# A decoder layer on one core: the order of pieces in the cross-attention

## What is computed

```python
q = jnp.einsum('btc,oc->bto', x, Wq) + bq            # x: (4, 1024, 256), 16 heads of 16
kv = jnp.einsum('bic,oc->bio', encoder_output, Wkv) + bkv   # 64 context vectors a batch
att = jnp.einsum('bhtd,bhid->bhti', q, k) * (1.0 / np.sqrt(D))
att = jax.nn.softmax(att, axis=-1)
y = jnp.einsum('bhti,bhid->bhtd', att, v)
y = y.transpose(0, 2, 1, 3).reshape(B, T, C)
return jnp.einsum('btc,oc->bto', y, Wo) + bo
```

## Time and profile before

| | us |
|---|---|
| median of 3 runs | 1554.58 |
| fastest and slowest run | 1554.28, 1557.01 |
| the profiled execution's own time | 1554.44 |
| its span, first to last instruction | 1552.5 |

### The profile page before, as it was taken

The page is one execution under the profiler, slowest core; times in us unless marked ns, Lnnn a source line. Parts: engine busy times, 40 slices in busy tenths (PEclk is TensorE's granted clock), DMA queues, the critical chain, the costliest instruction groups (busy, mean ns, idle before and its releaser), DMA issues. The chain is left out here.

```text
span 1552.5 us, 44246 instructions
## 1 busy us (share of the span) xinstructions
PE 1482.7 (96%) x18228; PEld 1091.7 (70%) x18228; DVE 1111.8 (72%) x1694; ACT 888.0 (57%) x1644; POOL 441.0 (28%) x633
## 2 busy tenths in 40 slices
PE   7999899978899999999999999999998999999997
PEld 4656666654536666666666666666657889999997
DVE  5787789857678898989898989898946633333332
ACT  2323677755638888888888888888882311111111
POOL 4110667644431111111111111111111124544543
PEclk9999999999999999999999999999999999999999
DMA  6000000002331111111111111111105765565562
GB/s 205 1 21 11 11 2 1 1 1 108 145 113 35 41 37 42 36 44 34 43 35 43 35 42 36 42 36 43 35 12 172 239 223 199 191 214 193 195 215 63
DMA packets 80078, 124.05 MB, mean 80 GB/s; under 512 B 22243, under 2 KB 46949, under 8 KB 79878
## 3 DMA queue, kind: packets, MB, share of 16 engines
q1 hardware_dynamic: 74262, 105.87, 22.7%
q0 software_dynamic: 5616, 15.34, 2.7%
HBM read 94.66 MB, written 26.08 MB: 78 GB/s over the span
## 5 line engine op out<-in xcount | busy, mean ns | idle before, releaser
L566 DVE TENSOR_REDUCE sb_m_mx<-banks 128x1 f32<-128x1024 f32 x512 | 603.9, 1220 | 76.6 <-PE banks L314 68.8
L485 ACT ACTIVATE sb_m_pT<-banks 128x512 f32<-128x512 f32 x1024 | 556.3, 595 | 110.6 <-PE banks L343 98.9
L343 PE MATMUL banks<-sb_m_q,sb_m_k 99*32 99x512 bf16 x4096 | 466.8, 380 | 2.2 <-DMA sb_m_q<-sb_m_mx_parts 1.3
L314 PE MATMUL banks<-sb_m_k,sb_m_q 96*32 96x512 bf16 x4096 | 359.9, 379 | 1.1 <-DMA sb_m_k<-k_parts 0.6
L358 PE MATMUL banks<-sb_m_pT,sb_m_v 128*32 128x256 f32 x4096 | 314.6, 379 | 0.7 <-ACT sb_m_pT L485 0.7
L343 PEld LDWEIGHTS banks<-sb_m_q,sb_m_k 99*32 99x32 bf16 x4096 | 178.6, 96 | 80.8 <-ACT sb_m_pT L485 6.1
L358 PEld LDWEIGHTS banks<-sb_m_pT,sb_m_v 128*32 128x32 f32 x4096 | 176.8, 109 | 58.9 <-ACT sb_m_pT L485 1.2
L314 PEld LDWEIGHTS banks<-sb_m_k,sb_m_q 96*32 96x32 bf16 x4096 | 159.0, 96 | 75.9 <-DVE sb_m_mx L566 6.3
L235 POOL CAST sb_m_mx_parts<-sb_m_mxT 8x128 bf16<-8x128 f32 x64 | 18.1, 283 | 574.8 <-issue 563.6
L2094 ACT ACTIVATE sb_e_hT<-banks 128x512 f32<-128x512 f32 x78 | 46.6, 597 | 234.8 <-PE banks L2052 234.8
L2052 PEld LDWEIGHTS banks<-sb_e_xT,w 128*128 128x128 f32 x1248 | 145.3, 192 | 3.4 <-DVE sb_e_xT L2104 1.5
(11 more groups left out here) (258 smaller groups left out, 1965.5 us busy)
## 6 DMA issues: line engine op xcount, KB each, us to landing
w<-in_w SPq DMA_DIRECT2D x47, 1024.0 KB, 5.1
sb_m_q<-q_parts SPq DMA_DIRECT2D x384, 32.0 KB, 1.8
sb_m_k<-k_parts SPq DMA_DIRECT2D x384, 32.0 KB, 1.8
q_parts<-sb_m_parts SPq DMA_DIRECT2D x24, 256.0 KB, 2.5
k_parts<-sb_m_parts SPq DMA_DIRECT2D x24, 256.0 KB, 2.4
X<-in_x SPq DMA_DIRECT2D x4, 1024.0 KB, 10.4
x_rows<-X SPq DMA_DIRECT2D x8, 512.0 KB, 8.5
z_rows<-sb_g_zs SPq DMA_DIRECT2D x8, 512.0 KB, 4.4
```

What stands on the lines that cost most here:

```text
L314: mm = pe.matmul(ps[2 * (k % 2) + h][c:c + 32, :], q_s[0:R, i, k * P + c:k * P + c + 32], k_s[0:R, i, h * 512:(h + 1) * 512], start=True, ...
L343: mm = pe.matmul(ps[rotating(use)][c:c + 32, :], k_s[:, i2, m * P + c:m * P + c + 32], q_s[:, i2, h * 512:(h + 1) * 512], start=True, stop ...
L485: act.activation(pT[:, m, h * 512:(h + 1) * 512], ps[rotating(f"b{m}{h}")][:, :], ACT.Exp).then_inc(exped, 1)
L566: dve.tensor_reduce(mx[:, par % 2, k:k + 1], pz[:, 2 * (k % 2):2 * (k % 2) + 2, :].rearrange("p q n -> p (q n)"), AX.X, ALU.max).then_inc( ...
```

## The change

Three orders change, and what goes with them:

- TensorE issues the scores of tile n + 1 instead of tile n at the head of slot n; those of tile 0 stand ahead of the loop.
- In a slot the turn now stands between scores and products, and the query between products and projection. Before, the query stood ahead of the products and the turn behind them. ScalarE's copies follow, and its normalization moves ahead of the copy of the products.
- VectorE computes the maxima of tile n ahead of the sums of tile n - 1. The subtraction stays behind them.

```diff
     def pieces_of(n):
         m = n // 2
         if n % 2 == 0:
-            first = [("query1", m + 1)] if m + 1 < PAIRS else []
-            return first, [("turn", m + 2)] if m + 2 < PAIRS else []
-        return [("query0", m + 2)] if m + 2 < PAIRS else [], []
+            queries = [("query1", m + 1)] if m + 1 < PAIRS else []
+            return [("turn", m + 2)] if m + 2 < PAIRS else [], queries
+        return [], [("query0", m + 2)] if m + 2 < PAIRS else []
...
+            score(0)
             for n in range(SLOTS):
-                if n < NT:
-                    score(n)
-                queries, turns = pieces_of(n)
-                for p in queries:
+                if n + 1 < NT:
+                    score(n + 1)
+                turns, queries = pieces_of(n)
+                for p in turns:
                     pe.wait_ge(piece_copied, NUMBER[p])
                     piece(p, ps[7])
                 if 0 <= n - 2:
                     products(n - 2)
-                for p in turns:
+                for p in queries:
                     pe.wait_ge(piece_copied, NUMBER[p])
                     piece(p, ps[7])
...
-                for p in queries:
+                for p in turns:
                     take(p, ps[7])
+                if g + 2 < NG:
+                    norm((g + 2) * GT + r)
                 if 0 <= n - 2:
                     act.wait_ge(pv, n - 1)
...
-                if g + 2 < NG:
-                    norm((g + 2) * GT + r)
-                for p in turns:
+                for p in queries:
                     take(p, ps[7])
...
+                if n < NT:
+                    dve.wait_ge(scores, n + 1)
+                    dve.tensor_reduce(mx[:, n % 2, :], sc, AX.X, ALU.max).then_inc(max_done, 1)
                 if 0 <= n - 1 < NT:
                     sums(n - 1)
                 if r == 0 and 0 < g and g + 2 < NG:
                     shift_of(g + 2)
                 if n < NT:
-                    sc = pz[:, 2 * (n % 2):2 * (n % 2) + 2, :].rearrange("p q (h n) -> p (q h) n", h=8)
-                    dve.wait_ge(scores, n + 1)
-                    dve.tensor_reduce(mx[:, n % 2, :], sc, AX.X, ALU.max).then_inc(max_done, 1)
                     need(dve, probsT, n - 1)
```

More of the change, by code:

```diff
@@ L1537, in _ @@
                 g, r = n // GT, n % GT
+                sc = pz[:, 2 * (n % 2):2 * (n % 2) + 2, :].rearrange("p q (h n) -> p (q h) n", h=8)
+                if n < NT:
+                    dve.wait_ge(scores, n + 1)
+                    dve.tensor_reduce(mx[:, n % 2, :], sc, AX.X, ALU.max).then_inc(max_done, 1)
                 if 0 <= n - 1 < NT:
```

## The result

The changed kernel took 1549.61 us (median of 11 runs, 1543.58 to 1553.04) against 1554.58 (11 runs, 1551.54 to 1557.21): a ratio of 0.9959, with 0.9950 to 0.9967 as its interval. That is 5.0 us faster: a small difference, but the interval leaves out 1. I had forecast 1.9 us less than the median before, too little to be told from no change.

A forecast was written before the change was run, and what follows sets the result against it. TensorE was taken to bound the pairs, and the ring of VectorE's sums, maxima, subtraction and ScalarE's exponential the last slots. Terms -2.6 + 0.1 + 2.5 + 0.4 - 2.1 = -1.7 us gave 1552.7 us, range 1549.4 to 1556.2.

The forecast's parts named there:

- 13 pairs: Two-slot pairs, slots 2 to 27: projection's 0.52 us wait hidden, new waits 0.20 and 0.12; -2.6 us.
- first slots: First two slots: TensorE waits there for tile 0's weights anyway; +0.1 us.
- slots behind the rounds: Closing rounds in slots 15, 19, 23, 27: VectorE waits for GpSimd's power, delaying maxima and sums; +2.5 us together.
- slots 19, 23, 27: Closing slots: ScalarE comes to the next copy of weights at 5.69 instead of 5.56; three times, +0.4 us.
- last slots: Slots without query or turn: 5.04 us become 4.30, and slot 32 gains another 0.45; -2.1 us together.
- The two new waits: TensorE in each pair: products wait 0.12 us for turned weights, query waits 0.20 for the copy of the turn.
- The cover of VectorE's waits: In the pairs TensorE is the bound, so moving VectorE's waits by the early maxima costs nothing; no value given.
- the ring: VectorE's sums, maxima, subtraction and ScalarE's exponential: 5.04 us a slot, bounding the last slots; opens with maxima beside the exponential.
- (a): Last slots: TensorE's low clock comes two slots early; +3.0 us at most, +1.5 as middle, 1554.2 us; chance 0.11.
- (b): Closing rounds absorbed: the 2.5 + 0.4 us are not paid; -4.6 us, 1549.8 us; chance 0.16.
- (c): No new wait at all on TensorE: -6.8 - 2.1 = -8.9 us, 1545.5 us; chance 0.05.
- (d): Closing rounds cost full price, 9.5 us instead of 2.5, and the kernel is slower: 1559.7 us; chance 0.07.

The follow-up runs named there:

- the pieces alone: Kernel before with only TensorE's turn and query and ScalarE's copies moved, scores and maxima as before: 1553.7 us, ratio 0.9994.
- narrow run: Changed kernel with an extra matmul of 32 stationary columns between query and projection in each slot: 1556.3 us, run once.
- wide: Changed kernel with an extra matmul of 128 stationary columns between query and projection in each slot: 1554.9 us, run once.
- the late shift: Changed kernel with VectorE's closing shift moved behind the sums of the next slot: 1545.26 us, ratio 0.9937.
- both edits: Changed kernel with closing shift behind the next slot's sums, turn ahead of scores, and the statistics' wait relaxed: 1547.75 us, ratio 0.9947.

## Why the prediction was wrong, step by step

```
term                          forecast   measured, us
13 pairs (10.48 before)       -2.6       13 x (9.78 - 10.48) = -9.1
first slots                   +0.1       -0.1
slots behind the rounds       +2.5       1.36 + 1.36 + 1.87 + 0.55 = +5.1
slots 19, 23, 27              +0.4       0.49 + 0.35 + 0.35 = +1.2
last slots                    -2.1       -0.13 - 0.73 - 0.74 - 0.45 = -2.1
sum                           -1.7       -5.0
```

(A term of the rounds is the slot behind the round and the one after it, against 5.20 and 4.57; for the last, slot 28 against its 5.24.) The clock, which the sum left out, gave 1.7 us at the transposes (slot 32 went from 8.16 to 6.04, 0.45 of it by the shorter wait) and took 1.9 behind them (from the last turning of weights to the stage behind 8.40 us, before 6.50). The sum was 3.3 us short, by two errors of opposite sign, 6.5 us in the pairs and 3.4 in the rounds. That the measured time still lies just above the lower end of my range, 1549.4, is luck.

**The pairs: the step that failed.** The layout took each piece's spacing from the order of before, "projection 3.51, weights 4.48" and "query 7.27, projection 8.33". Query and projection are 0.09 and 0.10 shorter each, four times 0.1 in a pair: they now stand side by side with weights of one shape, and the projection's copy is ready early. The products are 0.05 shorter in both slots, against 0.04 more for the turn. Part of what I had booked as work in the even slot before was waiting that no row lists: the turn at 207.39 and the projection at 207.94 each start 0.06 us behind the end of the copy they need (207.33 and 207.88). The two new waits were 0.12 and 0.16 us, as laid out. The waits were right, the work 0.5 us a pair too long, 6.5 us in all: the term of the pairs measured -9.1 us and not -2.6. The earlier trace rows alone doesn't show it. The rows of the weight loads hint at it, with their 0.33 us of unexplained idle time ahead of the products, and I had not read them.

**The cover of VectorE's waits: right only by luck.** "In the pairs this moves VectorE's waits, which were free" held for TensorE at 10.28. At 9.78 it would not: with the pieces alone the ring stops at about 10.2. The maxima, which I gave no value in the pairs, were worth 0.4 us a pair there.

**The rounds: right in mechanism, too small in size.** VectorE's wait, the order of what is queued behind it and the link over ScalarE's normalization are as forecast. Two slots behind a round take 11.13, 11.13 and 11.64 us, where the forecast had 10.28 + 0.47, + 0.83 and + 0.84, so 10.75, 11.11 and 11.12. The second is right in absolute time. Most of the difference to the measured loss I put down to this, that the chain of a round doesn't get shorter when TensorE does: 0.5 us of slack were gone in each. The narrow run bears this out: with pairs of 10.85 us its even slots behind the first three rounds are 5.74, 5.77 and 5.77, against 5.74 elsewhere. The third round has in addition the wait of 1.38 us for ScalarE's closing copies, which no step of mine had. For the same reason the slots 19, 23 and 27 lost 0.35 to 0.49 instead of 0.13.

**The last slots: right.** 4.30 us each, 2.15 from turning to products, and the 0.45 in slot 32 (329.59 - 323.55 = 6.04, in which products and projection follow as in the slots before).

**The rivals.** (a) did not happen: slots 31 and 32 left the clock up. (Of the waits that I set against it, the 1.12 us was VectorE's; TensorE's in those slots were 0.44 and 0.52. In the changed kernel it waits 1.11 twice, and the clock stays up.) (b), the rounds absorbed, gives 1549.8, nearly the time measured, and is false all the same: the rounds cost twice what I had said. (c) is false by the two waits, though its pairs of 9.96 us were still longer than the real ones: no case of mine had TensorE's own work shrink. (d) did not happen as priced, but the rounds cost 5.1 us of its 9.5, against my 2.5, and the slot behind the third takes 7.02.

## What to carry to other kernels

When pieces change places, look at the weight loads ahead of each group for idle time without a cause, and price each neighbour of another shape at what the trace shows for it (0.15 to 0.2 us here). Compare also the end of a copy with the start of the work that needs it: a start 0.06 us behind may be a wait that no row lists. When the bound engine gets faster, lay out the rings of the others against the new length, not the old: slack shrinks everywhere at once. Place a small VectorE instruction whose two inputs lie in SBUF where GpSimd is idle, not merely where its input is ready.

## What the runs showed of the hardware

- The first weight load of a group starts 0.21 us ahead of its matmul behind a group with weights of the same shape, if what it reads is ready (not at 207.93, where the copy had ended 0.05 us before). Behind one with 32 columns instead of 128 (narrow and wide) it doesn't, nor does that of the scores with their 64 rows. The query then takes 0.97 instead of 1.06 us, the projection 0.87 instead of 0.97, turning 0.88 instead of 0.97.
- VectorE's shift of 128x4 took 1.94 us instead of 0.16 while GpSimd's weighing of 1.90 us ran (once with the late shift, twice with both edits), 0.69 beside an addition, and 0.16 beside a power of four numbers.
- The stretches at the 1.2 GHz level differ from one execution to the next of the same program: added up over the span they are 38.5 us in the first trace of the changed kernel and 25.2 in the second. Its 11 runs go with the mean granted clock, from 1543.58 us at 0.993 to 1553.04 at 0.986. What starts such a stretch, with a wait of 2.10 us before it in one trace and the same wait without it in another, stays open.
